# Rows in the order (step, batch) for a fused attention, LSTM and FFN kernel: half of a token chain and seven of eight causal chunks placed inside the recurrence

## Chip, cores and metric

One NeuronCore of a Trainium2 chip runs the whole program. The metric is the device time of one execution in microseconds; the median of three runs of the kernel before is 687.82 us (687.6 to 689.17).

## What is computed

`x` is (4, 256, 128), `cond` (4, 128). Cut to its data flow:

```python
ada = cond @ w_ada + b_ada                       # 6 parts of 128, one set per batch
xm  = expmap0(layer_norm(logmap0(x)) * (1 + sc_msa) + sh_msa)
q, k, v = (to_heads(plin(xm, w, b)) for w, b in ...)     # 16 heads of 8
attn = softmax(logmap0(q) @ logmap0(k).T / sqrt(8))      # no mask: all 256 keys
x1  = mobius_add(x, expmap0(g_msa * logmap0(plin(from_heads(expmap0(attn @ logmap0(v))), w_o, b_o))))
xm  = expmap0(layer_norm(logmap0(x1)) * (1 + sc_mlp) + sh_mlp)
c   = mobius_add(x1, expmap0(g_mlp * logmap0(plin(plin(xm, w_f1, b_f1), w_f2, b_f2))))
x   = x + causal_attention(c)                            # low rank, c @ W_dkv @ W_uk and so on
a_t = x_t @ Wx + b + h @ Wh                              # 256 steps, 4 rows, h from cond, c = 0
c   = sigmoid(f) * c + sigmoid(i) * tanh(g);  h = sigmoid(o) * tanh(c)
out = x + gelu(h @ w1 + b1) @ w2 + b2
```

with `expmap0(v) = tanh(|v|) v / |v|`, `logmap0(x) = arctanh(|x|) x / |x|`, `plin(x, w, b) = expmap0(logmap0(x) @ w + b)`. The chain from the first attention's output to `c` acts on each token by itself. Step t of the recurrence needs `c` for tokens 0 to t of each batch, and nothing later.

## The kernel before

Each engine has one instruction list, written by hand; the lists meet through semaphores. The 1024 tokens lie in 8 tiles of 128 rows, tile 2b+k holding tokens 128k to 128k+127 of batch b.

- **Tables and statistics.** DVE takes the statistics of `x` (L675, L678), scales `ada_b` (L685), copies `cond` out of PSUM (L689). PE makes the six ada parts for each batch, one matmul with `ada_b` and one with `ada_w` into each bank (L1024, L1025), ACT copies them out (L525). Tiles are then turned (L1034) and multiplied by w_q, w_k, w_v (L1043). POOL, at the same time, clears `q_slab` (L450) and builds masks.
- **Head norms** (DVE L806 to L829), a split of q and k into f16 high and low parts (L838, L840), 64 turns (L1051), copies (ACT qS, DVE kS L843). Sixteen DMAs of SP put qS into the zeroed slab `q_slab`, a head's rows in a block of its own, so that all 128 rows can be contracted.
- **Attention 1.** 16 units of (group of four heads, batch): scores (L1066), exp on ACT (L554), values into four 32-column tiles of the array (L1078), turn back (L1089), `o_norm` on DVE.
- **The chain on all 8 tiles**: projection, `join` (L762), `front` (L714), two FFN products (L1137 to L1153), `join` again. Roots are Ln and Exp on ACT (`root`, L490 and L493) with three DVE instructions behind (`rsqrt`, L697 to L699); Ln, Exp and Tanh make ACT load tables (L515, L577).
- **Causal attention.** q, k, v (L1192's inputs; `qz` is filled by 16 more DMAs after POOL has cleared it, L459), then 16 first-half groups of units before the recurrence: scores L1192 and mask L1200, `m_max` L916, exp L611, four 128x128 turns on PE (L1210) and their copy (L923), values L1223, `m_norm`. The second half's units run inside the recurrence, one each 3 steps, through `pe_jobs`, `vec_jobs`, `act_jobs`.
- **Recurrence.** A step: gates on ACT (L642); DVE `pr` (L997), `h_fac` (L999), `gates` (L1001, the new cell); tanh on ACT (L644); DVE `h_off` (L1004), `h_low` (L1006) and `v_tm` (L1008, h for the FFN), then that step's jobs; on PE twelve matmuls (L1358) with `wha`, `whb` on `h_off` and `wha` on `h_low`, then that step's jobs. Each 32 steps the next inputs are made in the four last steps (`inputs_of`, L1242); the FFN pieces (`ffn_up` L1301, `ffn_down` L1316 and L1319, gelu L624) follow from the middle on.

What is queued behind `h_off` on PE, or stands in front of `pr` or `h_off` on DVE, is run first: a job is never overtaken.

Of the kernel before, what the change touches and what calls it, by code (L numbers as in the profile page):

```python
# [28 lines left out]
BF16 = mybir.dt.bfloat16  # L29

B, S, D, H = 4, 256, 128, 16
HD = D // H
FF = 512
P = 128
# [6 lines left out]

# [14 lines left out]
def _beta(a, b):  # L56
# [11 lines left out]
(X_SQ, ARG, IS_SMALL, LN_MINUS, LN_PLUS, N_SQ, ALPHA, V_FACTOR, NORM_SQ, U_NORM,  # L68
 XY, TANH_N, Y_FACTOR, Y_SQ, X_WEIGHT, U_WEIGHT, DENOM, F1_FACTOR, ROOT, NEWTON, GUARDED) = range(21)
SMALL_COLS = 21  # L70
# [8 lines left out]
BIAS_ROWS = BF16_PARTS * 4  # L79


def adaln_attention_lstm_ffn(nc, x, cond, w_q, b_q, w_k, b_k, w_v, b_v, w_o, b_o, w_f1, b_f1, w_f2, b_f2,
                             w_ada, b_ada, W_dq, W_uq, W_dkv, W_uk, W_uv, W_o, Wx, Wh, b_g, w1, b1, w2, b2, out):
    with ExitStack() as ctx:
# [19 lines left out]
        ada_b = sb("ada_b", [1, 6 * D])  # L104
        ada = sb("ada", [P, B, 6, D])
# [5 lines left out]
        bf1_all = sb("bf1_all", [P, FF])  # L111
# [9 lines left out]


# [8 lines left out]
        b2s = sb("b2s", [1, D])  # L131
        x_tb = sb("x_tb", [P, CHUNKS, D])


# [4 lines left out]
        x1_tm = sb("x1_tm", [P, TILES, D])  # L139
        o_tm = sb("o_tm", [P, TILES, D])  # L140
# [3 lines left out]
        qT = sb("qT", [P, TILES, P])  # L144
        kT = sb("kT", [P, TILES, P])
        qz = sb("qz", [P, H, B * S])


        pairs = qz[:].rearrange("p h n -> p (h n)").bitcast(F16)
        kS, qS = (pairs[:, i * NG * B * S:(i + 1) * NG * B * S].rearrange("p (g n) -> p g n", g=NG) for i in range(2))  # L150
        k_pair, q_pair = (pairs[:, i * TILES * H * SLOTS * HD:(i + 1) * TILES * H * SLOTS * HD].rearrange(
            "p (t h s d) -> p (t h) s d", t=TILES, s=SLOTS, d=HD) for i in range(2, 4))

        q_slab = pairs[:, H * B * S:].rearrange("p (h n) -> p h n", h=H)
        vaug = sb("vaug", [P, TILES, H, VP])
        hn = sb("hn", [P, 3, TILES, H])
        p_mla = sb("p_mla", [P, 2, 512])

        p_cond = [a[:].rearrange("p a t h d -> p a (t h d)")[:, i, :] for a in (q_sq, q_tm) for i in range(3)]
        oTs = sb("oTs", [P, 2, S])  # L160
        rd = sb("rd", [P, 2, HALVES, GROUP])
        rdm = sb("rdm", [P, 2, GROUP])
        small = sb("small", [P, SMALL_COLS, TILES])
# [46 lines left out]
        ada_ready = [sem("ada_msa_ready"), sem("ada_rest_ready")]  # L210
# [4 lines left out]
        v_ready = sem("v_ready")  # L215
# [104 lines left out]
        def flat(a):  # L320
            return a.rearrange("p t n -> p (t n)")
# [1074 lines left out]
```

## Time and profile before

| | |
|---|---|
| median of 3 runs | 687.82 us |
| the profiled execution: its span, first to last instruction (no other time is given for it) | 692.0 us |
| span against the median | 4.2 us more |
| start of the first gates, start of the last | 260.6 us, 683.8 us |
| busy PE, DVE, ACT, POOL | 463.2, 407.9, 234.5, 45.7 us |
| mean granted TensorE clock | 0.707 |

The profile's page gives busy shares of the whole span; the views by window, by line and by time give a stage. "idle before, releaser" is how long the engine sat before an instruction, and what it waited for last. An f32 matmul is recorded as two instructions, so "x8" of L1024 is four matmuls. The clock column is the granted share of TensorE's full 2.4 GHz.

### The profile page before, as it was taken

Reading aid. Unit: us, or ns where it says so; the run is one execution under the profiler, and the core shown is the slowest. Engines: PE = TensorE matmul, PEld = TensorE weight load, DVE = VectorE, ACT = ScalarE, POOL = GpSimd, SP = SyncE. Lnnn points to the kernel's source line nnn. Section 1 sums busy time; section 2 is a strip of 40 time slices with the busy share of each in tenths; the row PEclk is TensorE's granted clock in tenths of the full one; section 3 lists DMA queues with packets and bytes.
Section 4 is the critical chain, followed back from the end, with each engine's and each line's share of the span. In section 5 each row is a group of like instructions: output and inputs, shape, how many; then the busy total and the mean of one; then the engine's idle time right before and its main releaser. Section 6 shows DMA issues by size and latency. Waiting matters only on the chain.

```text
span 692.0 us, 13536 instructions
## 1 busy us (share of the span) xinstructions
PE 463.2 (67%) x5003; PEld 318.3 (46%) x5003; DVE 407.9 (59%) x2108; ACT 234.5 (34%) x818; POOL 45.7 (7%) x41
## 2 busy tenths in 40 slices
PE   0593799104839979888899889737367367367346
PEld 0231433102616756665566567536256246256334
DVE  6458533896674865767766775654444544544443
ACT  0023787232333523333433432223222232222222
POOL 9500002530000000000000000000000000000000
PEclk9997799655959985999985995555555555555555
DMA  7100200000002000000000000000000000000000
GB/s 188 45 0 0 61 2 2 0 0 0 1 0 32 1 1 2 1 3 1 2 1 3 1 2 1 2 1 1 5 6 2 5 6 1 5 5 3 5 1 5
DMA packets 9312, 7.00 MB, mean 10 GB/s; under 512 B 1845, under 2 KB 8093, under 8 KB 9246
## 3 DMA queue, kind: packets, MB, share of 16 engines
q1 hardware_dynamic: 8206, 5.60, 3.5%
q8 instruction: 40, 0.66, 0.4%
q10 hardware_dynamic: 1040, 0.52, 0.3%
q14 instruction: 26, 0.21, 0.1%
HBM read 4.02 MB, written 0.52 MB: 7 GB/s over the span
## 4 chain that ended last, share of the span: by engine, by line
PE 44%; DVE 36%; ACT 14%; issue 5%; DMA 1%; DVEq 0%
PE bank L1358 13%; ACT h_fac L644 6%; DVE h_off L1004 5%; PE bank L1192 5%; DVE pr L997 4%; ACT gates L642 4%; DVE gates L1001 4%; PE bank L1223 3%; PE bank L1078 3%; PE bank L1210 3%; DVE h_fac L999 2%; PE bank L1066 2%; DVE mx L916 2%; DVE q_sq L923 2%; DVE ada_b L685 2%
## 5 line engine op out<-in xcount | busy, mean ns | idle before, releaser
L1358 PE MATMUL bank<-h_off,wha 128*128 128x4 f16 x1020 | 68.3, 171 | 121.9 <-DVE h_off L1004 118.5
L1358 PEld LDWEIGHTS bank<-h_off,wha 128*128 128x128 f16 x1020 | 50.5, 106 | 166.4 <-DVE h_off L1004 160.7
L642 ACT ACTIVATE gates<-bank 128x16 f32<-128x16 f32 x256 | 46.9, 183 | 192.2 <-PE bank L1358 191.1
L997 DVE SCALAR_TENSOR_TENSOR pr<-gates 128x8 f32<-128x8 f32 x256 | 42.1, 164 | 106.3 <-ACT gates L642 106.3
L644 ACT ACTIVATE h_fac<-gates 128x4 f32<-128x4 f32 x256 | 53.1, 207 | 110.0 <-DVE gates L1001 110.0
L1004 DVE TENSOR_TENSOR h_off<-h_fac 128x4 f16<-128x4 f32 x256 | 43.3, 169 | 70.0 <-ACT h_fac L644 70.0
L1192 PE MATMUL bank<-kT,qz 128*128 128x128 f32 (+1 forms) x256 | 71.4, 394 | 0.0
L1358 PE MATMUL bank<-h_low,wha 128*128 128x4 f16 x1020 | 63.8, 167 | 0.0
L1358 PE MATMUL bank<-h_off,whb 128*128 128x4 f16 x1020 | 62.5, 166 | 0.0
L1006 DVE TENSOR_TENSOR_SCAN h_low<-h_fac,h_off 128x12 f16<-128x12 f32 x256 | 46.7, 183 | 8.7
L611 ACT ACTIVATE p_mla<-bank,mx 128x128 f32<-128x128 f32 (+1 forms) x128 | 44.4, 414 | 18.1 <-DVE mx L916 18.1
L1223 PE MATMUL bank<-q_sq,vaug 128*32 128x128 f32 x384 | 46.2, 312 | 1.9 <-DVE oTs L929 1.9
L1358 PEld LDWEIGHTS bank<-h_off,whb 128*128 128x128 f16 x1020 | 46.1, 101 | 0.0
L1358 PEld LDWEIGHTS bank<-h_low,wha 128*128 128x128 f16 x1020 | 45.8, 103 | 0.0
L1192 PEld LDWEIGHTS bank<-kT,qz 128*128 128x128 f32 x256 | 38.8, 209 | 7.1 <-issue 7.0
L1210 PE MATMUL bank<-ident,p_mla 128*128 128x128 f32 x192 | 41.3, 315 | 0.9 <-ACT p_mla L611 0.9
L999 DVE TENSOR_SCALAR h_fac<-gates 128x4 f32<-128x4 f32 x256 | 41.3, 161 | 0.0
L1001 DVE SCALAR_TENSOR_TENSOR gates<-pr 128x4 f32<-128x4 f32 x256 | 41.3, 161 | 0.0
L1008 DVE TENSOR_TENSOR v_tm<-h_fac 128x4 f32<-128x4 f32 x256 | 37.1, 145 | 0.0
L923 DVE COPY q_sq<-bank 128x512 f32<-128x512 f32 x48 | 32.9, 686 | 5.2 <-PE bank L1210 5.2
L916 DVE TENSOR_REDUCE mx<-bank 128x2 f32<-128x512 f32 (+1 forms) x48 | 32.9, 686 | 4.8 <-PE bank L1200 4.6
L1210 PEld LDWEIGHTS bank<-ident,p_mla 128*128 128x128 f32 x192 | 24.1, 157 | 9.4 <-issue 5.5
(224 smaller groups left out, 737.9 us busy)
## 6 DMA issues: line engine op xcount, KB each, us to landing
qz<-qz SPq DMA_DIRECT2D x16, 64.0 KB, 2.0
x_tm<-in_x ACTq DMA_DIRECT2D x1, 512.0 KB, 5.0
wf<-in_L_cond_w_f SPq DMA_DIRECT2D x2, 256.0 KB, 5.7
x_tb<-in_x SPq DMA_DIRECT2D x4, 128.0 KB, 2.7
qz<-qT SPq DMA_DIRECT2D x16, 32.0 KB
out_y<-tb SPq DMA_DIRECT2D x7, 64.0 KB, 1.9
ada_w<-in_L_cond_w_ada SPq DMA_DIRECT2D x1, 384.0 KB
bf_all<-in_L_cond_b_f SPq DMA_DIRECT2D x1, 256.0 KB, 5.8
```

The costliest lines, as they stand in the source:

```text
L642: nc.scalar.activation(gates[:, k, 0:GW], src, ACT.Tanh, scale=1.0 / A_SCALE).then_inc(gates_act, 1)
L644: nc.scalar.activation(h_fac[:, k, :, 1], gates[:, 1 - k, 4 * B:5 * B], ACT.Tanh, scale=0.5).then_inc(th_act, 1)
L916: V.tensor_reduce(mx[:, m % 2, 0:512 // n], bank[:, m % 2, :].rearrange("p (j n) -> p j n", n=n), AX.X, ALU.max, negate=True).then_inc(mx_ ...
L923: V.tensor_copy(pt_mla[:, m % 2, :], bank[:, 2 + m % 2, :]).then_inc(mt_ready, 1)
L997: V.scalar_tensor_tensor(pr[:, k, :], gates[:, k, B:3 * B], 1.0, gates[:, k, 3 * B:5 * B], ALU.add, ALU.mult).then_inc(p_ready, 1)
L999: V.tensor_scalar(h_fac[:, k, :, 2], gates[:, k, 0:B], 1.0, 0.5 * H_SCALE, ALU.add, ALU.mult)
L1001: V.scalar_tensor_tensor(gates[:, 1 - k, 4 * B:5 * B], pr[:, k, B:2 * B], 0.5, pr[:, k, 0:B], ALU.mult, ALU.add).then_inc(c_new, 1)
L1004: V.tensor_tensor(h_off[:, k, :, 2], h_fac[:, k, :, 2], h_fac[:, k, :, 1], ALU.mult).then_inc(h_ready, 1)
L1192: T.matmul(bank[:, m % 2, j * n:(j + 1) * n], qz[:, h, b * S + half * P:b * S + half * P + P], kT_flat[:, b * S:b * S + n], start=(j == 0) ...
L1210: ins = T.transpose(bank[:, 2 + m % 2, i * P:(i + 1) * P], p_mla[:, m % 2, i * P:(i + 1) * P], ident[:])
L1223: ins = T.matmul(bank[VP * j:VP * j + VP, 4, 0:P], vaug[:, HALVES * b + kc, h, :], pt_mla[:, m % 2, i * P:(i + 1) * P], start=(kc == 0), s ...
L1358: ins = T.matmul(acc[:, g * B:(g + 1) * B], w[:, g, :], h, start=False, stop=True, skip_group_check=True)
```

## The change

The chain on half k (tokens 128k and on) becomes a generator `side(k)` per engine. `side(0)` runs among the second 16 units of attention 1 and after them; `side(1)` is carried as far as tables of step numbers say (`VEC_AT`, `ACT_AT`, `PE_AT`, `Pace`), most of it inside steps 0 to about 70. Its tiles are 32 steps by 4 batches (`x_tb` order), so a tile is one chunk of causal attention (`attend(c, i)`); chunk 0 comes ahead of the recurrence, chunks 1 to 7 inside.

```diff
+CHUNK_FROM = {1: 0, 2: 20, 3: 40, 4: 64, 5: 88, 6: 112, 7: 136}
+VEC_AT = dict(second=0, joined=0, log1=12, log2=15, moved=25, v_ready=36, squared0=38, squared1=40, squared2=42, squared3=45,
+              f1_factor=49, fed=53, third=60, fourth=65)
+PE_AT = dict(projected=30, v_turned=33, up0=34, up1=37, up2=39, up3=43, normed=45)
...
-            for k, (a, z) in enumerate(ADA_PARTS):
...
-                    T.matmul(y, ones[:], ada_b[:, a:z], start=True, stop=False)
-                    ins = T.matmul(y, condR[:, bb], ada_w[:, a:z], start=False, stop=True)
+            for bb in range(B):
+                ins = T.matmul(bank[:, 1 + bb // 2, bb % 2 * 2 * D:(bb % 2 + 1) * 2 * D], condR[:, bb], ada_w[:, 0:2 * D], start=True, stop=True)
...
+            T.matmul(bank[:, 3, :], condS[:].rearrange("p t b -> p (t b)"), ada_w[:, 2 * D:6 * D], start=True, stop=True).then_inc(ada_mm, 1)
```

(`ada_b` is now spread over 128 rows by a DMA of ACT's queue and added on DVE as the tables are copied out.) POOL no longer clears `q_slab` and `qz`, and SP's 32 DMAs into them are gone; folding of the second attention's weights, the turns of `x_tb` and the product with `Wx` move ahead of attention 1.

```diff
 # attention 1, scores and values
-                    ins = T.matmul(bank[:, 2 * (w % 2) + kc, :], kS[:, g, ...],
-                                   q_slab[:, h:h + 2, bb * S:(bb + 1) * S], start=True, stop=True)
+                        ins = T.matmul(bank[:, 2 * (w % 2) + j % 2, i * P:(i + 1) * P], kS[rows, g, ...],
+                                       qS[rows, g, bb * S + k * P:bb * S + (k + 1) * P], start=True, stop=True,
+                                       tile_position=(SLOTS * HD * j, 0), skip_group_check=True)
 # a root: was Ln and Exp on ACT and three DVE instructions
+                    on(V.tensor_scalar(at(y).bitcast(I32), at(a).bitcast(I32), -0.5, ROOT_BITS, ALU.mult, ALU.add))
+                    on(V.tensor_tensor(at(T1), at(a), at(y), ALU.mult))
+                    on(V.scalar_tensor_tensor(at(T1), at(T1), -ROOT_K, at(y), ALU.mult, ALU.mult))
+                    on(V.scalar_tensor_tensor(at(T2), at(T1), ROOT_C, at(y), ALU.add, ALU.mult))
+                    on(V.tensor_tensor(at(T1), at(a), at(T2), ALU.mult))
+                    on(V.scalar_tensor_tensor(at(T1), at(T1), -1.0 / ROOT_S ** 2, at(T2), ALU.mult, ALU.mult))
+                    on(V.scalar_tensor_tensor(at(Y), at(T1), 10.0 / 3.0, at(T1), ALU.add, ALU.mult))
+                    on(V.scalar_tensor_tensor(at(y), at(Y), 5.0, at(T2), ALU.add, ALU.mult))
 # causal attention: turns of p
-                    ins = T.transpose(bank[:, 2 + m % 2, i * P:(i + 1) * P], p_mla[:, m % 2, i * P:(i + 1) * P], ident[:])
+                V.transpose(pt_mla[:, m % 2, n * part:n * (part + 1)], p_mla[:, m % 2, n * part:n * (part + 1)]).then_inc(mt_ready, 1)
 # the recurrence on DVE
                 V.scalar_tensor_tensor(gates[:, 1 - k, 4 * B:5 * B], ...).then_inc(c_new, 1)
+                rest.go(t, 1)
                 vec.wait_ge(th_act, t + 1)
                 V.tensor_tensor(h_off[:, k, :, 2], h_fac[:, k, :, 2], h_fac[:, k, :, 1], ALU.mult).then_inc(h_ready, 1)
...
-                for job in vec_jobs(t):
-                    job()
+                for c, i in attending(t):
+                    attend(c, i)
+                    jobs += 1
+                rest.go(t, 3 if jobs == 0 else 2)
```

A log is now bits, a fit and two Exp steps, so ACT needs no Ln. The diff of PE's causal scores: one matmul of 32(c+1) columns for four heads (32 rows of the array) and a 32-column mask matmul; its values: 36-column matmuls on a block-diagonal V (`vbd`), four batches in four 32-column tiles. The twelve matmuls and six DVE instructions of a step are the same (now L1622 and L1291 to L1302; gates L760, tanh L762). `hist` is what `v_tm` was.

Where instructions move, on PE in attention 1. Before, scores and values alternate by batch (`qz` is the storage that the slab and kS share, `vaug` V, `q_sq` and `q_tm` exponentials):

```order
L1066 MATMUL bank<-qz 128x512 x2
L1078 MATMUL bank<-q_sq,vaug 32x256 x4
L1066 MATMUL bank<-qz 128x512 x2
L1078 MATMUL bank<-q_sq,vaug 32x256 x2
L1078 MATMUL bank<-q_tm,vaug 32x256 x2
```

and now, in the second 16 units, with half 0's turns and projection (L1422, L1427, L1434) between:

```order
L1398 MATMUL bank<-q_tm,vaug 32x128 x8
L1427 MATMUL bank<-ident,o_tm 128x128 x4
L1380 MATMUL bank<-qS,kS 128x128 x8
L1398 MATMUL bank<-q_tm,vaug 32x128 x8
L1434 MATMUL bank<-wo_c,vT 128x128 x4
L1380 MATMUL bank<-qS,kS 128x128 x8
```

One score product of 512 columns on the full array has become four of 128 columns on a quarter of its rows.

PE in the recurrence, steps 34 to 37. Before, a step that turns and takes values (L1210, L1223), then scores:

```order
L1358 MATMUL bank<-h_low,wha 128x4 x4
L1210 MATMUL bank<-ident,p_mla 128x128 x3
L1223 MATMUL bank<-q_sq,vaug 32x128 x3
L1358 MATMUL bank<-h_off,wha 128x4 x4
L1358 MATMUL bank<-h_off,whb 128x4 x4
L1358 MATMUL bank<-h_low,wha 128x4 x4
L1223 MATMUL bank<-q_sq,vaug 32x128
L1192 MATMUL bank<-kT,qz 128x256
L1197 MATMUL bank<-mask,identb 128x128
```

and now (L1446 is the first FFN product of half 1, L1496 a chunk's values):

```order
L1622 MATMUL bank<-h_low,wha 128x4 x4
L1478 MATMUL bank<-kT,qz 128x96
L1480 MATMUL bank<-mask,sel 128x32
L1478 MATMUL bank<-kT,qz 128x96
L1480 MATMUL bank<-mask,sel 128x32
L1622 MATMUL bank<-h_off,wha 128x4 x4
L1622 MATMUL bank<-h_off,whb 128x4 x4
L1622 MATMUL bank<-h_low,wha 128x4 x4
L1496 MATMUL bank<-vbd,pt_mla 32x36 x12
L1446 MATMUL bank<-vT,wf 128x512
L1622 MATMUL bank<-h_off,wha 128x4 x4
```

The step's own matmuls keep their order; what stands behind `h_low` is other work.

DVE in a step, before with a causal unit's two jobs, and now with a chunk's and the chain's (L1109 the chain, L1247 a turn of p):

```order
L1001 SCALAR_TENSOR_TENSOR gates<-pr 128x4
L1004 TENSOR_TENSOR h_off<-h_fac 128x4
L1006 SCALAR_TENSOR_TENSOR h_low<-h_fac,h_off 128x12
L1008 TENSOR_TENSOR v_tm<-h_fac 128x4
L923 COPY q_sq<-bank 128x512
```

```order
L1294 SCALAR_TENSOR_TENSOR gates<-pr 128x4
L1109 SCALAR_TENSOR_TENSOR sm<-sm 128x4
L1298 TENSOR_TENSOR h_off<-h_fac 128x4
L1300 SCALAR_TENSOR_TENSOR h_low<-h_fac,h_off 128x12
L1302 TENSOR_TENSOR hist<-h_fac 128x4
L1247 STREAM_TRANSPOSE pt_mla<-p_mla 128x128
L1109 SCALAR_TENSOR_TENSOR sm<-sm 128x4 x2
```

A chain instruction now stands between the new cell and `h_off`, where there was none.

## Rows read from the trace of the kernel before

**Rows 1.** Busy time in stretches: span; engines; granted clock; DMA share, GB/s.
```profile
0.00:53.70 53.70, 28.98 (x47) 11.02 (x48) 30.14 (x71) 8.21 (x19) 26.22 (x33) 1.00 0.30 75
53.70:79.40 25.70, 10.28 (x76) 7.73 (x74) 21.53 (x35) 13.04 (x18) 0.00 (x0) 0.67 0.05 12
79.40:121.20 41.80, 40.29 (x358) 13.22 (x356) 13.46 (x50) 33.10 (x33) 3.82 (x1) 1.00 0.08 19
121.20:205.40 84.20, 28.46 (x155) 20.14 (x155) 66.37 (x204) 26.39 (x66) 15.67 (x8) 0.65 0.00 0
...
260.60:683.80 423.20, 300.33 (x3936) 225.53 (x3937) 241.44 (x1651) 131.44 (x608) 0.00 (x0) 0.63 0.01 3
683.80:692.00 8.20, 4.91 (x20) 3.27 (x20) 1.27 (x8) 1.20 (x6) 0.00 (x0) 0.50 0.04 10
```
**Rows 2.** The same, two stretches of the recurrence.
```profile
280.00:340.00 60.00, 52.17 (x691) 35.99 (x690) 43.89 (x267) 23.39 (x100) 0.00 (x0) 1.00 0.01 2
...
415.00:450.00 35.00, 31.29 (x323) 21.09 (x321) 20.81 (x129) 10.11 (x45) 0.00 (x0) 0.50 0.01 1
```
**Rows 3.** Timeline, one step without jobs: start, duration (us), engine, idle before, releaser.
```profile
500.89 0.19 PEld L1358 LDWEIGHTS bank<-h_off,wha 128*128 128x128 f16 x4 [1.20 <-DVE h_off L1004]
...
501.41 0.18 ACT L642 ACTIVATE gates<-bank 128x16 f32<-128x16 f32 x1 [0.78 <-PE bank L1358]
501.63 0.17 DVE L997 SCALAR_TENSOR_TENSOR pr<-gates 128x8 f32<-128x8 f32 x1 [0.51 <-ACT gates L642]
...
502.26 0.17 DVE L1004 TENSOR_TENSOR h_off<-h_fac 128x4 f16<-128x4 f32 x1 [0.27 <-ACT h_fac L644]
```
**Rows 4.** Timeline, a step whose PE jobs are long.
```profile
441.53 1.06 PE L1223 MATMUL bank<-q_sq,vaug 128*32 128x128 f32 x6
...
442.52 0.18 PEld L1358 LDWEIGHTS bank<-h_off,wha 128*128 128x128 f16 x4 [0.38 <-issue]
...
443.04 0.18 ACT L642 ACTIVATE gates<-bank 128x16 f32<-128x16 f32 x1 [1.33 <-PE bank L1358]
```
**Rows 5.** Timeline of DVE, the start.
```profile
5.72 1.64 DVE L675 BATCH_NORM_STATS2 st<-x_tm 128x6 f32<-128x128 f32 x8 [5.72 <-DMA x_tm<-in_x]
```
**Rows 6.** Groups of instructions by line and form, 0 to 53.7 us.
```profile
L450 POOL MEMSET qz<- 128x1024 f16 x16 | 14.4, 947 | 0.0
L685 DVE TENSOR_SCALAR ada_b<-ada_b 1x128 f32<-1x128 f32 x1 | 13.7, 13666 | 0.0
```
**Rows 7.** Timeline of PE, the ada tables.
```profile
24.36 1.22 PE L1024 MATMUL bank<-ada_b,ones 1*128 1x256 f32 x2 [18.09 <-DVE condR L689]
...
33.56 2.07 PE L1024 MATMUL bank<-ada_b,ones 1*128 1x512 f32 x2
```
**Rows 8.** Timeline, attention 1.
```profile
90.51 0.11 PEld L1066 LDWEIGHTS bank<-qz 128*128 128x128 f16 x2 [0.41 <-issue]
...
91.05 0.64 PE L1078 MATMUL bank<-q_sq,vaug 128*32 128x256 f32 x8
...
92.52 1.02 ACT L554 ACTIVATE q_tm<-bank 128x1024 f32<-128x1024 f32 x1 [0.34 <-PE bank L1066]
```
**Rows 9.** Timeline of DVE, the chain's first join.
```profile
125.91 5.25 DVE L764 TENSOR_SCALAR small<-small 128x8 f32<-128x8 f32 x1
131.74 0.17 DVE L697 TENSOR_TENSOR small<-small 128x8 f32<-128x8 f32 x1 [0.58 <-ACT small L493]
131.94 0.17 DVE L698 SCALAR_TENSOR_TENSOR small<-small 128x8 f32<-128x8 f32 x1
...
132.55 2.19 DVE L768 SCALAR_TENSOR_TENSOR ta<-ta,small,ada 128x128 f32<-128x128 f32 x8
```
**Rows 10.** Groups by line and form, 262 to 450 us.
```profile
L916 DVE TENSOR_REDUCE mx<-bank 128x2 f32<-128x512 f32 x32 | 21.9, 683 | 0.0
...
L929 DVE COPY oTs<-bank 128x128 f32<-128x128 f32 x15 | 4.2, 283 | 0.0
```
**Rows 11.** Timeline, the first step's matmuls, with the unsplit f32 `wh`.
```profile
258.84 1.71 PE L1358 MATMUL bank<-h,wh 128*128 128x4 f32 x8
```

More of the change, by code:

```diff
@@ new lines, in _ @@
+            exps(0, PER_HALF)
+            exps(16, 18)
+            first, second = side(0), side(1)
+            until(first, "turned")
+            exps(18, 19)
+            until(first, "first")
+            exps(19, 20)
+            until(first, "second")
+            o_copy(0)
+            exps(20, 22)
+            until(first, "bent")
+            exps(22, 24)
+            o_copy(1)
+            exps(24, 27)
+            until(first, "log1")
+            exps(27, 28)
+            until(first, "log2")
@@ L574, in _ @@
+            for i in range(chunk_span(0)):
+                attend(0, i)
+                if i == 8:
+                    until(second, "second")
             act.wait_ge(w_ready, 6)
@@ L802, in _ @@
+            for k in range(2):
+                vec.wait_ge(sq_out, 1 + k)
+                go(V.tensor_reduce(half(col(V_FACTOR), k), half(tb, k), AX.X, ALU.add))
+            done()
+            step(V.tensor_scalar(col(GUARDED), col(V_FACTOR), TINY, None, ALU.max), roots_in)
+            rsqrt(col(GUARDED), col(V_FACTOR), col(NEWTON))
+            step(V.tensor_scalar(col(V_FACTOR), col(V_FACTOR), CLIP, 1.0, ALU.mult, ALU.min))
             vec.wait_ge(ld_qkv, 96)
@@ new lines, in _ @@
+            until(first, "v_ready")
+            for f in range(FC):
+                until(first, f"squared{f}")
+                if f == 1:
+                    until(second, "normed0")
+            until(second, "normed1")
+            until(first, "f1_factor")
+            until(first, "fed")
+            until(second, "normed3")
+            until(first, "fourth")
+            until(second, "added")
+            until(first, "end")
+            go(V.memset(h_fac[:], 0.0))
+            go(V.memset(h_off[:], 0.0))
@@ L962, in _ @@
+            for i in range(chunk_span(0)):
+                attend(0, i)
+            until(second, "second")
             step(V.memset(gates[:], 0.0), c_new)
@@ L1263, in _ @@
-            pe.wait_ge(mv_ready, 1)
+            pe.wait_ge(kT_ready, NG)
+            pe.wait_ge(qT_ready, NG)
+            pe.wait_ge(vaug_ready, 1)
+            first, second = side(0), side(1)
+            scores(0)
+            scores(1)
+            for g in range(NG):
+                units(PER_GROUP * g, PER_GROUP * g + 2)
+                if g:
+                    until(first, f"turn{g - 1}")
+                units(PER_GROUP * g + 2, PER_GROUP * (g + 1))
+            until(first, f"turn{NG - 1}")
```

1578 lines of the change are left out of this document (907 added, 671 removed).

## Prediction

> **What bounds the kernel now.** I read the stretches first, then the timeline of one step, then groups and timelines of the earlier stages. The stretches [rows 1] split the span of 692.0 us in two: 260.6 us before the first gates, and 423.2 us for 255 intervals of the recurrence, with a tail of 8.2 us. Outside attention 1 no engine fills the first part: DVE is the busiest, with 66.4 of the 84.2 us of the token chain, where small instructions follow each other; PE has 28.5 there. That work can only be shortened or put where an engine idles. The reader is to see in a step without jobs [rows 3] where it idles: the gates repeat after 1.60 us whatever the clock, because each engine waits for the next; PE stood idle for 1.20 us (1.27 from its last h matmul to the next `h_off` by my reading of start times), ACT .78, DVE .51 ahead of `pr` and .27 ahead of `h_off`. Over 255 intervals PE alone has some 320 us of room. An interval is prolonged only by what exceeds such a gap: the job of 1.06 us in [rows 4], begun late, holds the h matmuls ([0.38 <-issue]) and the next gates come 1.33 us after the last ACT work in place of .78. All intervals together exceed 255 x 1.594 = 406.5 us by 16.7, all of it in stretches at clock .50: in one at 1.00, with PE busy for 52.2 of 60 us, none did [rows 2]. So the sum is: time to the first gates, plus 406.5, plus overruns, plus tail.
>
> **The tables (a gain of 28).** Now PE's first table product waits until 24.4 [rows 7] for DVE's scaling of `ada_b`, which took 13.7 us beside POOL's 16 memsets of 14.4 us [rows 6]; these are removed. In the new order the statistics and copies end at about 10.1 (x lands at 5.7 and its statistics take 1.64 [rows 5]; then .64 for their sums, three copies and small work). Then four products of 256 columns at 1.15 (eight of them from 24.36 to 33.56) and one of 512 at 2.0 [rows 7], where sixteen took 25.1, give 16.7; sums with the bias, normalisation and turns 9 us. QKV starts at 25.7 for 53.7: -28.
>
> **Up to attention 1 (+1.5).** The 25.7 us of this stretch [rows 1] keep their DVE work; ten weight turns and products go into PE's idle 15 us. Their ACT and DVE copies, and 2.7 us of statistics of `x_tb`, stand ahead of the last k copies. Start of the scores: 53.3.
>
> **Attention 1, first half and its output (31).** Each half has 16 exps of 1.02 us [rows 8], so ACT needs 16.4. PE's values of a (group, batch) cost .55 twice for four column tiles at a time (91.05 to the next score product, less its gap). Now eight matmuls of 128 columns alternate between two of the tiles, which I take as two at a time: .85; scores on 32 rows .21 to .43. With the gaps of both changes 1.3 us per unit, 21; fill 4; the last turns, norm, turn and projection 6. The chain's input stands at 84.2. A score product contracted 128 rows before, three quarters of them zeros of the slab; now 32.
>
> A rule speaks against this part. The row shows PE idle for .41 us at issue where 32-column values give way to scores [rows 8], and the same .38 in the recurrence [rows 4]; both are in my 1.3. The Trainium skill ("TensorEngine Tiling (Array Packing)", section Key Properties) says that a change of tiling mode, not of tile, drains TensorE. By that rule each tiled job in the recurrence pays a change too: the overruns counted below at half clock are 65 us with .25 us for each such step, and 57 without, so the sum would be 6 us lower if the rule did not hold here. This case's rows agree in that the gap stands at the change, but cannot tell it from a weight load's wait.
>
> **The chain for four tiles (75).** Small chained instructions repeat each .20 us, 128x8 or less alike [rows 9]; per-tile ones cost 2.19 / 8 = .275. The collision with POOL's memset of `qz` (5.25 us for an instruction of .17) goes. A root was two ACT instructions with two crossings (.58 of the second is seen in [rows 9]) and three on DVE, some 1.3 us, and is now eight on DVE: 1.6. The removed table loads I cost at nothing, as ACT waits there. Join: 33 small, 16 per-tile, one reduction and squares with crossings: 13.5. Front: 48 small, 8 per-tile, 8 of statistics and two Exp crossings: 12.5. Clip and scaling 4.4. FFN: two products of four tiles, at 2.19 per tile and a factor: 15.4; the second half's `o_norm` lies between. Join again 13.7. Ends at 143.7; the second half's first part, 12 small and 8 per-tile, which is not overlapped, 5.1: 148.8.
>
> **Chunk 0 (9) and entry (4).** Four units, each a round of scores, maximum, exp, turns and values of some 2.2 us when nothing else runs, behind one tile's turn and projections: reductions of up to .68 [rows 10], turns of p on DVE. No row before has such a turn; between .28 (copy of 128x128) and .68 (128x512) [rows 10], I take .28, the same shape. Then norm, turn, inputs 1.8, and `wh` 1.71 [rows 11]. First gates: 162 for 260.6, 99 earlier; 157 at full clock.
>
> **The recurrence.** 406.5 stays. I added, per step of the new lists, PE's jobs against 1.27, DVE's behind `hist` against .51, its one instruction ahead of `h_off` (.20 to .22) against .27, ACT's against .80. Prices: a 512-column f32 product 1.7 to 2.0 at half clock (by [rows 7], whose pace is that of the long jobs at .50) and half of that at full; 128 columns f32 .35 ([rows 4], three in 1.06) to .43; small DVE work .20. Overruns: 65 us at half clock, of which 31 by t = 63 (there each of 4 up products of 1.7 and 16 + 16 narrow f32 ones meets chunk 1's and 2's scores), 16 in t 64 to 159 and 18 behind; 32 at full clock, mostly DVE's. In it .25 in each step with tiled matmuls stands for the gap at issue, below the .38 seen; without it the half-clock count is 57. The clock was .50 in most of the recurrence before [rows 1], mean .63, though at 1.00 in the loaded stretch. By that mean three quarters of steps go at half clock: 56. But jobs that come late in one step leave the next with more room, which a sum by step does not see: before, such a sum would have given more than the 16.7 found. I take 48. Tail: the last piece is unchanged, 8.2.
>
> **Sum.** 162 + 406.5 + 48 + 8.2 = 624.7 us of span. The profiled execution before has 692.0 against a median of 687.8, so I take off 4.2: **620.5 us**, 67 less.
>
> **Rivals.**
> (a) *The clock stays up in the loaded stretches.* For it: [rows 2] 1.00 for 60 us with causal work. Against: the new steps carry less PE work each. Then entry at 157 and overruns near 32: 157 + 406.5 + 32 + 8.2 - 4.2 = 600.
> (b) *Half clock throughout, nothing absorbed.* All of 65: 637.5. If also the value tiles of attention 1 run one after another, 1.70 for .85 over 16 units, 13 more: 651. For it: PE is idler than before; against: the 16.7 of before.
> (c) *Slower.* The chain's instruction between the new cell and `h_off`, and the waits at the head of chunk jobs, stand in the path of each step: DVE's list cannot pass them. If such an instruction waits for PE or ACT work that is itself queued behind the h matmuls, each affected interval grows by up to an engine round, .8 us. To bring back 67 us on top of the 48, a mean of .26 us over all 255 intervals is needed, or .8 us in 84 of them. Against: chunks are active in most steps, but their waits are two or more steps after the producer, and the DVE gap holds .20 in .27. Then 620.5 + 67 + 1 = 689.
> (d) *The recurrence absorbs it, the front does not:* stream turns of .68, tiny tiled matmuls at issue cost, chunk 0 and the log's crossings at twice my price: +15: 636.
> (e) *The chain of half 1 is not hidden, only moved.* Alone it takes 75 us as half 0's; if none fits the gaps, its 31 us of overruns before t = 64 become 75: 664. Against: .20 in .27 and three times .20 against .51 leave only .1 over per step.
>
> **How the numbers follow.** My case .44, (a) .2, (b) .15, (d) .14, (e) .02, (c) .05, of which .01 ends within the noise. A measurement here tells about 0.3%, 2 us. The range that leaves 2 in 10 out: down to 597 (case (a) with its entry costs a little lower), up to 648, between the two ends of (b). Faster .95, same .01, slower .04, as every case but (c) is over 30 us to that side.
>
> **What would show it.** First gates near 162; QKV from 25.7; no POOL memset beside DVE's first instructions; an attention unit of 1.3 us; gates 1.60 apart in steps without jobs; overruns in t 33 to 50 and at steps with 4c score columns, released by PE at clock .50. I am wrong if first gates lie 10 us off, if intervals without PE overrun still exceed 1.65 (then DVE's inserted instruction is in the path), or if the stretch of t 75 to 250 adds more than 35 us.

## The result and the profile after

The changed kernel takes **647.08 us** (median of 4, 645.41 to 648.18) where the kernel before took 688.50 in the same comparison; ratio .9382, interval .9356 to .9409. That is 41 us less; 67 were forecast (620.5 us), and the value lies 1 us inside the range's upper end. On three later chips the kernel before took 676 to 682 us in 7 of 25 executions and 687 to 695 us in the others, so the four here are of its longer kind, and against the shorter ones the changed kernel gains 32 us (645.7 for 677.9 on one chip, ratio .9519, interval .9478 to .9561), less than half of the 67 forecast.

The page, and below it the stretches of the profile after (span, PE, PEld, DVE, ACT, POOL busy, clock), which answer to [rows 1]:

```profile
span 644.5 us, 16323 instructions
...
PE 489.7 (76%) x6317; PEld 383.3 (59%) x6317; DVE 385.3 (60%) x2265; ACT 239.7 (37%) x928; POOL 20.5 (3%) x31
...
PEclk9567996886555555565555555555565555556555
```

```profile
0.00:26.30 26.30, 6.67 (x19) 4.46 (x20) 22.60 (x74) 4.24 (x11) 13.28 (x25) 0.82 0.58 158
26.30:54.00 27.70, 15.55 (x62) 9.71 (x63) 25.05 (x43) 16.84 (x31) 6.09 (x5) 0.62 0.00 1
...
85.00:130.00 45.00, 32.59 (x394) 22.89 (x392) 25.49 (x131) 21.61 (x49) 0.00 (x0) 0.77 0.01 1
130.00:177.80 47.80, 35.02 (x248) 29.79 (x242) 28.36 (x126) 16.69 (x73) 1.15 (x1) 0.67 0.00 1
177.80:636.30 458.50, 367.77 (x5138) 292.31 (x5138) 273.78 (x1860) 159.25 (x742) 0.00 (x0) 0.51 0.01 3
636.30:644.50 8.20, 4.85 (x20) 3.21 (x19) 1.07 (x7) 1.15 (x6) 0.00 (x0) 0.50 0.01 2
```

The last three numbers of a stretch are clock, DMA share and GB/s. An interval is the time from one step's gates to the next step's, and its overrun is what it has above the 1.594 us of a step without jobs. The first gates come at 177.8 us, not 260.6: 82.8 us earlier, of 99 forecast. The recurrence takes 458.5 us for 423.2, so 35.3 us are given back: its overruns are 52.0 us for 16.7. The tail is the same 8.2. So the change took about 83 us out of the front and paid back 35 inside, which is the shape that was forecast. The mean clock of the recurrence is .51, where it was .63.

Where the 52.0 us stand can be read from the start times of each step. Some 35 us lie between `h_off` and PE's first h matmul, where PE is still at a job. Some 11 us lie ahead of `pr`, where DVE is still at its own jobs, and 2.7 us ahead of `h_off`, behind the chain's inserted instruction.

Two long intervals show how the work is paid for. First PE, at step 43, with half 1's norm products of one column:

```profile
257.63 0.25 PE L1622 MATMUL bank<-h_low,wha 128*128 128x4 f16 x4
257.80 0.59 PE L1496 MATMUL bank<-vbd,pt_mla 128*32 128x36 f32 x24
259.23 0.27 PE L1622 MATMUL bank<-h_off,wha 128*128 128x4 f16 x4 [0.84 <-DVE h_off L1298]
259.36 0.25 PE L1622 MATMUL bank<-h_off,whb 128*128 128x4 f16 x4
259.47 0.25 PE L1622 MATMUL bank<-h_low,wha 128*128 128x4 f16 x4
259.56 3.49 PEld L1452 LDWEIGHTS bank<-ones,q_pair 128*128 128x128 f32 x16
259.58 3.55 PE L1452 MATMUL bank<-ones,q_pair 128*128 128x1 f32 x16
262.99 0.25 PE L1622 MATMUL bank<-h_off,wha 128*128 128x4 f16 x4
```

Twelve value matmuls of 36 columns (257.80) leave PE idle for .84 us before the next step. Eight products of one column (259.58, two records each) take 3.55 us, .43 each, and the weight queue is busy for 3.49 us of that, so one column costs what 128 do in the prediction (.35 to .43), and the rows point to the loading of the 128x128 weights. The next h matmuls wait for them and the interval is 3.73 us. Then step 34, where causal scores and a first FFN product (L1446) meet:

```profile
240.19 2.08 PE L1446 MATMUL bank<-vT,wf 128*128 128x512 f32 x2
242.05 0.29 PE L1622 MATMUL bank<-h_off,wha 128*128 128x4 f16 x4
...
242.60 0.18 ACT L760 ACTIVATE gates<-bank 128x16 f32<-128x16 f32 x1 [1.94 <-PE bank L1622]
242.81 0.17 DVE L1291 SCALAR_TENSOR_TENSOR pr<-gates 128x8 f32<-128x8 f32 x1 [2.50 <-ACT gates L760]
```

ACT and DVE both wait behind PE, DVE 2.50 us for .51 in [rows 3]. The interval is 3.59 us.

The overruns of the kernels are compared in the table at the end of the experiments.

### The profile page after: what moved, and what is told of

Read it like the earlier page. It is cut to its first block, busy times and chain, and to the rows that moved or that the text cites. A ratio compares the mean times of both kernels' runs of the same rounds, so it can differ in the third digit from the quotient of the medians.

```text
span 644.5 us, 16323 instructions
## 1 busy us (share of the span) xinstructions
PE 489.7 (76%) x6317; PEld 383.3 (59%) x6317; DVE 385.3 (60%) x2265; ACT 239.7 (37%) x928; POOL 20.5 (3%) x31
## 4 chain that ended last, share of the span: by engine, by line
PE 44%; DVE 33%; ACT 16%; issue 5%; DMA 1%; PEldq 0%; ACTq 0%; DVEq 0%
PE bank L1622 14%; PE bank L1478 6%; ACT h_fac L762 6%; DVE h_off L1298 5%; ACT gates L760 5%; DVE pr L1291 4%; PE bank L1398 4%; DVE gates L1294 4%; DVE h_fac L1292 2%; DVE mx L1237 2%; PE bank L1518 2%; DVE pt_mla L1247 2%; PE bank L1446 2%; PE bank L1380 2%; PE bank L1460 2%
## 5 line engine op out<-in xcount | busy, mean ns | idle before, releaser
L1622 PEld LDWEIGHTS bank<-h_off,wha 128*128 128x128 f16 x1020 | 52.0, 109 | 145.2 <-DVE h_off L1298 135.8
L1622 PE MATMUL bank<-h_off,wha 128*128 128x4 f16 x1020 | 68.9, 172 | 84.0 <-DVE h_off L1298 80.0
L760 ACT ACTIVATE gates<-bank 128x16 f32<-128x16 f32 x256 | 47.2, 185 | 181.2 <-PE bank L1622 181.0
L1291 DVE SCALAR_TENSOR_TENSOR pr<-gates 128x8 f32<-128x8 f32 x256 | 41.5, 162 | 112.4 <-ACT gates L760 111.6
L1478 PE MATMUL bank<-kT,qz 32*128 32x32 f32 (+7 forms) x256 | 105.8, 534 | 0.0
L762 ACT ACTIVATE h_fac<-gates 128x4 f32<-128x4 f32 x256 | 53.1, 207 | 120.2 <-DVE gates L1294 120.2
L1478 PEld LDWEIGHTS bank<-kT,qz 32*128 32x128 f32 x256 | 63.6, 311 | 3.1 <-issue 1.1
L1622 PE MATMUL bank<-h_low,wha 128*128 128x4 f16 x1020 | 63.4, 167 | 0.0
L1622 PE MATMUL bank<-h_off,whb 128*128 128x4 f16 x1020 | 62.7, 166 | 0.0
L1622 PEld LDWEIGHTS bank<-h_low,wha 128*128 128x128 f16 x1020 | 46.8, 104 | 0.0
L1622 PEld LDWEIGHTS bank<-h_off,whb 128*128 128x128 f16 x1020 | 46.7, 103 | 0.0
L706 ACT ACTIVATE p_mla<-bank,mx 128x32 f32<-128x32 f32 (+7 forms) x128 | 43.3, 368 | 6.0 <-DVE mx L1237 6.0
L1496 PE MATMUL bank<-vbd,pt_mla 128*32 128x36 f32 x1152 | 40.0, 254 | 4.7 <-ACT qS L731 3.8
L1302 DVE TENSOR_TENSOR hist<-h_fac 128x4 f32<-128x4 f32 x256 | 37.1, 145 | 0.0
L1247 DVE STREAM_TRANSPOSE pt_mla<-p_mla 128x192 f32<-128x192 f32 (+5 forms) x96 | 35.5, 369 | 2.0 <-ACT p_mla L706 1.7
L1496 PEld LDWEIGHTS bank<-vbd,pt_mla 128*32 128x32 f32 x1152 | 33.0, 157 | 6.0 <-issue 4.0
L1237 DVE TENSOR_REDUCE mx<-bank 128x2 f32<-128x320 f32 (+7 forms) x48 | 26.3, 549 | 3.9 <-PE bank L1480 3.7
L1480 PE MATMUL bank<-mask,sel 32*128 32x32 bf16 x128 | 28.6, 225 | 0.0
```

The costliest lines, as they stand in the source:

```text
L706: ins = nc.scalar.activation(p_mla[:, m % 2, i * n:(i + 1) * n], bank[:, 3 + m % 2, i * n:(i + 1) * n], ACT.Exp, bias=mx[:, m % 2, i:i + 1])
L760: nc.scalar.activation(gates[:, k, 0:GW], src, ACT.Tanh, scale=1.0 / A_SCALE).then_inc(gates_act, 1)
L762: nc.scalar.activation(h_fac[:, k, :, 1], gates[:, 1 - k, 4 * B:5 * B], ACT.Tanh, scale=0.5).then_inc(th_act, 1)
L1247: V.transpose(pt_mla[:, m % 2, n * part:n * (part + 1)], p_mla[:, m % 2, n * part:n * (part + 1)]).then_inc(mt_ready, 1)
L1291: V.scalar_tensor_tensor(pr[:, k, :], gates[:, k, B:3 * B], 1.0, gates[:, k, 3 * B:5 * B], ALU.add, ALU.mult).then_inc(p_ready, 1)
L1478: T.matmul(bank[:, 3 + m % 2, i * n:(i + 1) * n], qz[rows, c % 2, bs[i]].rearrange("p j t -> p (j t)"), kT[rows, bs[i], 0:n], start=(i == ...
```

## Experiments

Twelve runs on three chips; those of one group share a chip: e1 to e4, e5 to e8, e9 to e12. The program's time is its span plus 1.8 us, in all executions but two of e7 (2.3 and 3.2). Executions of one changed kernel lay 1 to 12 us apart. So the kernels are compared by their own intervals, and by medians against the changed kernel's 645.7 (e9) to 647.1. The changed kernel was run beside e10 to e12 alone: for e1 to e8 a difference of 1 to 3 us between medians is not told apart from one between chips, and the overruns decide.

**e1, the instruction ahead of `h_off` taken away.**

```diff
-                rest.go(t, 1)
-
                 vec.wait_ge(th_act, t + 1)
...
-                rest.go(t, 3 if jobs == 0 else 2)
+                rest.go(t, 4 if jobs == 0 else 3)
```

> The chain's one DVE instruction between the new cell and h_off is taken away; all of the chain's DVE work stands behind hist (up to 4 instructions a step). Overrun theory (PE jobs at half clock): the gap ahead of h_off holds .20 in .27, so nothing is won there, and four chained instructions of .20 exceed the .51 behind hist by .3 in some 35 steps: 5 to 12 us slower than the changed kernel (652 to 659 us). Rival (the inserted instruction stands in the path): steps 0 to 70 get shorter, 5 us or more faster (below 642 us).

Measured 648.11 us (645.39 to 651.63), overruns 55.7 for 52.0, and all the increase is in t below 96. On the whole the instruction is cheaper where it stood, and nothing like the loss of rival (c) is there. DVE of the changed kernel, a step with it:

```profile
196.05 0.16 DVE L1294 SCALAR_TENSOR_TENSOR gates<-pr 128x4 f32<-128x4 f32 x1
196.13 0.15 DVE L1102 SCALAR_TENSOR_TENSOR sm<-sm 128x4 f32<-128x4 f32 x1
196.49 0.17 DVE L1298 TENSOR_TENSOR h_off<-h_fac 128x4 f16<-128x4 f32 x1 [0.20 <-ACT h_fac L762]
```

DVE still waits .20 for tanh behind it (.27 without), so a small instruction is free there. A large one is not. In step 36 a product of 128x512 stands in that place:

```profile
244.71 0.16 DVE L1294 SCALAR_TENSOR_TENSOR gates<-pr 128x4 f32<-128x4 f32 x1
244.79 0.68 DVE L1180 TENSOR_TENSOR q_pair<-k_pair 128x512 f32<-128x512 f32 x1
245.39 0.16 DVE L1298 TENSOR_TENSOR h_off<-h_fac 128x4 f16<-128x4 f32 x1
```

Tanh starts at 244.91, so `h_off` follows it by .48 us for the usual .24. In e1 steps 36, 38, 40 and 42 fall from 1.84 to between 1.60 and 1.69, and step 49 from 2.25 to 1.59. Rival (c)'s mechanism is real in nine steps of the changed kernel, and costs 2.7 us there. In e1 these 2.7 are gone, but the waits ahead of `pr` grow by some 7 us. The loss was forecast too high, 5 to 12 us for 3.7 by the overruns.

**e2, values over two steps.**

```diff
+                    if c and (kb <= c // 2) != (half == 0):
+                        continue
...
-                    m_values(c, u)
+                    m_values(c, u, 0)
+                if c and w == 1 and 0 <= u < unit_count(c):
+                    m_values(c, u, 1)
```

> A causal unit's value matmuls of chunks 1 to 7 are spread over two steps, half of the key blocks in each. Overrun theory: the 10 longest steps behind t = 64 (2.3 to 3.15 us, some 11 us over) are value jobs that meet another job; halved, 6 to 10 us less than the changed kernel (637 to 641 us). Rival (waits between engines, not PE's load, make these steps long): within 2 us of 647.

647.73 us (646.96 to 650.17), overruns 56.1. The longest steps fell (134: 2.99 to 2.63 us, 162: 3.11 to 2.75), but steps that had been at 1.6 now took 1.9 to 2.2, for the second half lands where the next unit's scores are. The expectation was wrong: I had looked at peaks. A cycle of three steps has 3.8 us of room, and PE is recorded busy for 45.5 of the 50 us from 450 to 500 us, which holds the first of these steps.

**e3, POOL's bias work after k's turns.**

```diff
+            pool.wait_ge(k_turned, NG)
             pool.wait_ge(w_ready, 4)
```

> POOL's six bias conversions wait until k is turned, and so no longer run beside DVE's q, k and v products (1.39 us for .56, 3.61 for 2.36, 1.62 for 1.22). Theory that POOL slows DVE there: 2.5 us less, 644.5 us, first gates 2.5 us earlier. Rival (the long durations are the instructions' own): no change, and DVE's rows as before.

644.27 us (640.03 to 646.63), first gates at 174.2. DVE and POOL, in the changed kernel and then in e3:

```profile
42.08 1.17 POOL L517 TENSOR_TENSOR bg<-bg,p_mla 1x512 f32<-1x512 f32 x1
42.28 1.39 DVE L901 SCALAR_TENSOR_TENSOR hn<-hn,nq 128x384 f32<-128x384 f32 x1
43.70 3.61 DVE L904 SCALAR_TENSOR_TENSOR q_tm<-q_tm,hn 128x1024 f32<-128x1024 f32 x2
47.23 1.62 DVE L907 TENSOR_TENSOR vaug<-q_tm,hn 128x1024 f32<-128x1024 f32 x1
```

```profile
41.99 0.56 DVE L902 SCALAR_TENSOR_TENSOR hn<-hn,nq 128x384 f32<-128x384 f32 x1
42.59 2.36 DVE L905 SCALAR_TENSOR_TENSOR q_tm<-q_tm,hn 128x1024 f32<-128x1024 f32 x2
44.87 1.22 DVE L908 TENSOR_TENSOR vaug<-q_tm,hn 128x1024 f32<-128x1024 f32 x1
55.58 0.60 POOL L515 CAST p_mla<-bg 1x512 bf16<-1x512 f32 x1 [40.07 <-PE bank L1369]
```

The same three instructions take 4.1 us for 6.6, and the split of k into high and low parts starts at 48.20 for 50.98. The change removed POOL's long memsets from DVE's side and put small POOL work beside these three products. The DVE rows show 2.5 to 2.8 us; the rest of the earlier gates is within what one profile differs from another (175 to 180 us over the other kernels), and the median alone, on another chip, would not show it.

**e4 and e5, the clock.** Filler matmuls on PE in steps 60 to 189, into a bank that nothing reads there (e4: 128 columns each; e5: 512 columns, with `wha` in place of the second `identh`, the sum of jobs and filler higher).

```diff
+                for _ in range(FILL[t]):
+                    T.matmul(bank[:, 0, 0:P], identh[:], identh[:], start=True, stop=True, skip_group_check=True)
```

> In steps 60 to 189 PE's idle time behind the jobs is filled with matmuls of 128 columns f16 on the identity into an unused bank (up to 10 of .107 us, so that jobs and filler come to some 1.15 us at half clock). Nothing of the result changes. Theory that idleness keeps the clock at .50: it rises to 1.00 in a part of that stretch, and its overruns (some 20 us at half clock) fall to some 10: 637 us. Rival (the clock does not follow such work): clock .50 as before, and no change or up to 5 us slower from filler that begins late.

> As the last filler, but with matmuls of 512 columns on the full array, so that jobs and filler of a step in 60 to 189 come to 1.75 us at half clock, above the 1.27 of room. Theory that the clock follows the columns that PE moves: it rises to 1.00 as it did in 280 to 340 us of the kernel before; then filler and jobs fit the room, that stretch's overruns fall from 21 to some 10 us, and the sum is near 637. Rival (the clock stays at .50 in this stretch whatever PE does): each of 130 intervals grows by up to .5 us, 690 us or more.

e4: 648.13 us, e5: 669.2 us (664.71 to 676.77). Stretches of the changed kernel, e4 and e5:

```profile
320.00:360.00 40.00, 29.88 (x432) 23.49 (x432) 22.97 (x161) 13.29 (x63) 0.00 (x0) 0.50 0.01 1
450.00:500.00 50.00, 45.51 (x668) 34.43 (x666) 31.21 (x191) 17.63 (x77) 0.00 (x0) 0.53 0.01 2
```

```profile
320.00:360.00 40.00, 38.84 (x528) 32.59 (x525) 22.40 (x157) 12.76 (x61) 0.00 (x0) 0.50 0.01 2
450.00:500.00 50.00, 47.86 (x681) 36.58 (x681) 30.38 (x188) 17.91 (x78) 0.00 (x0) 0.50 0.01 2
```

```profile
320.00:360.00 40.00, 37.96 (x523) 22.71 (x521) 23.81 (x166) 13.68 (x65) 0.00 (x0) 0.98 0.01 2
450.00:500.00 50.00, 49.54 (x635) 32.78 (x632) 28.04 (x175) 15.94 (x70) 0.00 (x0) 0.64 0.01 2
```

With the wide filler the clock did go up, to .98 in 320 to 360 us, and there the steps between 74 and 101 were all within 1.7 us though they carry more work (in the changed kernel step 78 takes 2.28 and step 92 takes 1.99). With the narrow one, for which PE is recorded just as busy, it stayed at .50, and e4's rival held. But with the wide filler the clock was down to .78 in 360 to 400 us, then .64 and .50, and then the filler itself overran: t 128 to 191 went from 13.1 us to 29.4. So the clock of this recurrence can be raised for a while, but not kept up, and not at this price. Both theories of e5 were too simple: it was neither 637 nor over 690.

**e6, chain first in ACT's and PE's lists ahead of the recurrence.**

```diff
-            exps(24, 27)
-            until(first, "log1")
-            exps(27, 28)
-            until(first, "log2")
+            exps(24, 25)
+            until(first, "log1")
+            exps(25, 26)
+            until(first, "log2")
+            exps(26, 28)
...
-            units(18, 31)
+            units(18, 29)
             until(first, "v_turned")
             until(first, "up1")
-            units(31, 32)
+            units(29, 32)
```

> ACT's exps of the second half of attention 1 stand behind the chain's two log exps where they stood ahead of them, and PE turns half 0's chain and makes its first FFN products ahead of the last three units, not behind all but one. Theory that chain and attention hold each other up in the two lists (DVE waits of 2.64 and .78 us for ACT, 7.6 us ahead of the squares): first gates 3 to 5 us earlier than 177.8, 642 to 644 us. Rival (PE's and ACT's sums bound this stretch, whatever the order): within 1 us.

644.49 us (643.33 to 646.73) but first gates at 178.4, not earlier: the rival held, as far as one profile can tell. It is the profile of the longest of e6's four executions, and the others were 1.3 to 3.4 us shorter, so a small gain is not excluded. Waits moved from the log to the FFN: DVE's wait of 2.64 us is gone, and the one of 7.59 ahead of the squares is 9.72.

**e7, half 1's FFN spread over more steps** (each first product in two of 256 columns, four norm matmuls a step, two second products a step, later tables, `CHUNK_FROM` 70, 94, 118, 142, `FFN_EVERY` 7).

```diff
-CHUNK_FROM = {1: 0, 2: 20, 3: 40, 4: 64, 5: 88, 6: 112, 7: 136}
+CHUNK_FROM = {1: 0, 2: 20, 3: 40, 4: 70, 5: 94, 6: 118, 7: 142}
...
+                            if k and f == 1:
+                                yield
```

> Half 1's FFN products in steps 33 to 54: each first product in two of 256 columns in two steps, four norm matmuls a step for eight, two second products a step for four; what follows of the chain and chunks 4 to 7 come 6 steps later. The matmul work is the same. Overrun theory: the six steps of 2.8 to 3.84 us (34, 37, 39, 43, 44, 46; 10.7 us over) fall to about 2.2 each, others rise by .3: 4 to 7 us less, overruns of t 32 to 63 near 12 for 17.4; 641 to 643 us. Rival (PE's sum over these 20 steps is full, as the split of the values showed behind t = 64): no gain, 645 to 649.

650.04 us (649.38 to 653.14), overruns 57.0, t 32 to 63 21.1 for 17.4. Steps 43 and 44 did fall to 2.03 and 2.13, and 50 and 55 rose to 4.07 and 3.81, where parts meet chunk 2's and 3's. The rival held, and there was a loss beside.

**e8, masks behind pairs of scores.**

```diff
                              start=(i == 0), stop=True, skip_group_check=True, tile_position=(32 * g, 0))
+                for i in range(len(bs) // 2 * part, len(bs) // 2 * (part + 1)):
                     ins = T.matmul(...sel32[rows, :], mask32[rows, :], ...)
```

> Two causal score matmuls, then their two masks, where score and mask alternate; same work. In chunk 0 a pair of 32 columns repeats each .48 us though its columns are few. Theory that the change between f32 scores and bf16 masks costs (a drain at each): chunk 0 shorter by up to 2 us and two changes fewer in each score step of the recurrence, 3 to 6 us less in all. Rival (the pair is bound by its three weight loads, .18 to .33 each): no change within 1 us.

643.05 us (642.55 to 644.35), overruns 51.0. PE in chunk 0 of the changed kernel, then of e8:

```profile
163.31 0.61 PE L1478 MATMUL bank<-kT,qz 32*128 32x32 f32 x2
163.73 0.21 PE L1480 MATMUL bank<-mask,sel 32*128 32x32 bf16 x1
163.79 0.61 PE L1478 MATMUL bank<-kT,qz 32*128 32x32 f32 x2
```

```profile
161.71 0.44 PE L1519 MATMUL bank<-w_mla,coT 128*32 128x128 f32 x4
162.08 1.06 PE L1478 MATMUL bank<-kT,qz 32*128 32x32 f32 x4
...
163.03 1.06 PE L1478 MATMUL bank<-kT,qz 32*128 32x32 f32 x6
```

A pair takes .48 us alternating and .95 us for two in e8: the same. Changing between f32 and bf16 costs nothing in chunk 0. That the price is the three weight loads of a pair is the rival's reading, and no run tests it. In the recurrence the order matters a little: steps 34 and 37 fell by .14 each and steps 51, 52, 55, 64 and 65 by .2, step 47 rose by .5, and all overruns fell by 1.0. What the median shows beyond that is not explained by a row.

**e9 to e12.** e9 is the changed kernel itself. In e10 DVE adds the four squared blocks, and 4 norm products replace 16; the tables move them to step 45:

```diff
+                        ins = V.tensor_tensor(f1q[:, 0], f1q[:, 0], f1q[:, f], ALU.add)
...
-                for f in range(FC):
-                    pe.wait_ge(f1_sq, FC * k + f + 1)
-                    for c in range(SIDE):
+                pe.wait_ge(f1_sq, k + 1)
+                for c in range(SIDE):
```

e11 is e10 with e3's and e8's edits. In e12 PE makes only a stub of half 1's FFN inside the recurrence, and leaves the rest of it out:

```diff
+                    n = 16 if k else 4 * P
...
-                    for c in range(SIDE):
+                    for c in range(1 if k else SIDE):
...
-                    for f in range(FC):
+                    for f in range(1 if k else FC):
```

> The changed kernel as it is, beside the three below on one chip. By every theory as before: 645 to 648 us, overruns of the 255 intervals 52 us.

> The squares of the FFN's four blocks are added on DVE (three adds of .69 us for each half), so that PE makes 4 norm products with one column in place of 16, .43 us each at half clock. Same result up to rounding. Overrun theory: steps 43 and 44 (3.73 and 3.84 us) fall to one of some 2.3, 3 to 4 us less in t 32 to 63, of which DVE's adds give back about .5; before the recurrence 16 products of .23 us become 4, up to 2 us more less DVE's three adds (2.1 us, if they are in the path). Sum: 2 to 5 us less than the changed kernel beside it. Rival (the room is used up everywhere, what leaves one step comes back in the next, as with the two splits): within 1 us.

> Norms summed, the pairs of masks behind the pairs of scores, and POOL's bias work after k is turned, together. If the three add up: 6 to 9 us less than the changed kernel beside it, near 639 us.

> Half 1's FFN is left out on PE but for a stub in the recurrence (first products of 16 columns for 512, 4 norm matmuls for 16, 4 second products for 16); its result is wrong. Overrun theory: t 32 to 63 fall from 17.4 us over to about 5, the rest unchanged: 12 us less than the changed kernel. Rival (the chain's DVE and ACT work or waits on it are what prolongs these steps): 3 us less at most.

| | median us (range) | first gates | overruns, us | of which t 32 to 63 |
|---|---|---|---|---|
| before | 677.89 (677.47 to 680.75) in three, 690.45 (687.80 to 690.82) in eight | 260.6 | 16.7 | 1.0 |
| changed, first time | 647.08 (645.41 to 648.18) | 177.8 | 52.0 | 17.4 |
| e9 changed | 645.69 (643.78 to 648.26) | 176.8 | 52.0 | 17.4 |
| e10 norms summed | 642.47 (640.49 to 644.04) | 175.5 | 48.5 | 13.8 |
| e11 all three | 635.90 (631.65 to 641.12) | 176.9 | 47.1 | 13.3 |
| e12 stub | 635.86 (633.73 to 637.81) | 179.3 | 42.0 | 7.7 |

(First gates and overruns are from one profile each; those of before from the first one.) e9 repeats the overruns to a tenth. e12 shows that half 1's FFN on PE is 9.7 of the 17.4 us of steps 32 to 63 (forecast: about 12), and its median is 9.8 us below e9's. e10 turns two steps of 3.73 and 3.84 into 2.32 and 2.63 and is 3.2 us faster by medians, within the 2 to 5 forecast; its step 45, with four norm products behind a unit's values:

```profile
261.16 0.25 PE L1626 MATMUL bank<-h_low,wha 128*128 128x4 f16 x4
261.34 0.58 PE L1500 MATMUL bank<-vbd,pt_mla 128*32 128x36 f32 x24
261.86 1.87 PE L1458 MATMUL bank<-ones,q_pair 128*128 128x1 f32 x8
263.58 0.25 PE L1626 MATMUL bank<-h_off,wha 128*128 128x4 f16 x4
```

**e11 beats both kernels**: 635.9 us, 9.8 less than the changed one beside it (6 to 9 forecast) and 42 to 55 less than the kernel before. Each of its six executions is shorter than each of the changed kernel's six. Its overruns give 4.9 of the 9.8 and POOL's place some 2.7, if it is worth there what it was in e3; the last two are not shown by a row, and its profiled execution (638.8 us of span) was one of its longer ones.

## Why the prediction was right, and by how much it was off

**The mechanism holds, the number only just.** The front is shorter, the recurrence is prolonged mostly by PE jobs at clock .50, and the base step and the tail are untouched. But the time is 27 us above the forecast, and it is inside the range by 1 us only because the range reached up to the middle of rival (b), whose serial value tiles did not come. That is luck. Two of the prediction's own signs of being wrong came true: the first gates lie 15.8 us off, where 10 were allowed, and 37 intervals exceed 1.65 us though PE was not late (11.9 us of overrun, nearly all behind DVE's work). The 27 us fall on three terms.

**The front, 15.8 us too small.** *Tables*: QKV at 26.3 for a forecast of 25.7. *Up to attention 1*: scores at 58.5 for 53.3; I costed DVE's products at their old durations and did not see POOL's bias work move beside them, which e3 measures at 2.5 to 2.8 us. The other 2 us of this stretch are not accounted for. *Attention 1*: 33.0 us for 30.9; a unit is 1.33 us at full clock, as taken, and the value matmuls do overlap (1.07 us for eight, between the .85 taken and the 1.70 of rival (b)), but one unit, at half clock, took 2.4 us, and each fourth is followed by turns. *The chain*: its heading says 75 us, and rival (e) uses that number, but its parts and the sum (84.2 to 148.8) come to 64.6. It took 71.4, from 91.5 to 162.9. Both joins and the second half's part were right within .2 us. The front took 15.7 us for 12.5 and the FFN 19.6 for 15.4. I had summed DVE's instructions and PE's products as if alone, while the second half of attention 1 stands between them in the same lists:

```profile
109.60 0.94 DVE L1109 SCALAR_TENSOR_TENSOR sm<-sm 128x4 f32<-128x4 f32 x5
113.18 0.16 DVE L1114 TENSOR_TENSOR sm<-sm 128x4 f32<-128x4 f32 x1 [2.64 <-ACT sm L637]
...
114.79 0.16 DVE L1127 TENSOR_TENSOR sm<-sm 128x4 f32<-128x4 f32 x1 [0.78 <-ACT sm L637]
...
132.20 1.42 DVE L1180 TENSOR_TENSOR q_pair<-k_pair 128x512 f32<-128x512 f32 x2 [7.59 <-ACT k_pair L651]
```

DVE waits 2.64 us for an Exp of .22 that stands behind three attention exps, 2.88 us together, in ACT's list. That e6 moves these waits and its first gates come no earlier suggests that the two streams together bound this stretch. Chunk 0 and the entry took 14.8 us for 13.2. Rival (d) had 15 us more for the front, which is the size that came, but for other reasons: the turns of p took .24 in chunk 0, not .68, and of its reasons only the log's crossings are in these rows.

**The recurrence, 4 us.** 52.0 against 48. The count by steps was 65 us at half clock with an allowance for a change of tiling, and 57 without. Two choices failed in opposite ways. The clock was not high for a quarter of the steps but for almost none (.51), so it is case (b) in the clock. And the allowance of .25 us for a change of mode was not there. I had read [.41 <-issue] and [.38 <-issue] in [rows 4, 8] as PE's idle time; it stands in the row of the weight queue. PE itself went on: in the trace before, the score product that begins at 90.51 is recorded for .61 us, and the values of [rows 8] start at 91.05, while it is still at work. In the changed kernel values on 32 columns follow `h_low` by .17 us (257.63 to 257.80), where a product on the full array follows it by .11 (259.47 to 259.58), and scores on 32 rows start while the last projection on 32-column tiles is recorded (161.71 + .44, and 162.08, in e8). The rule of the Trainium skill ("TensorEngine Tiling (Array Packing)", Key Properties) that a change of tiling mode drains TensorE may hold, but by these rows the change to tiles costs some .06 us, not .25; no row separates the change back.

The count with the allowance had 31 us by t = 63, 16 in t 64 to 159 and 18 behind; the trace has 23.7, 14.7 and 13.6. Without the allowance 5 us remain between 57 and 52. That late jobs find room in the next step is my reading of them; no run shows it. One cost was taken as nothing and was not: the inserted instruction was counted at .20 to .22 against a gap of .27, but four of them are products of .68 us, and 2.7 us come of such ones (e1).

**The reference to the median, 6.8 us.** I took 4.2 us off the span, because the profiled execution before had 692.0 against a median of 687.8. But an execution's time is its span plus 1.8: that profile was of an execution 6 us above the median. The changed kernel has no execution that far from its median, so the correction had the wrong sign: 1.8 should have been added, not 4.2 taken off, and the changed kernel's median lies .8 above its profiled execution.

**Rivals.** (a) failed, though e5 shows the clock at .98 when PE is given more. (b) came in the clock, but not with its 65 us nor with its serial value tiles. (c) failed in size: its mechanism is there in nine steps, for 2.7 us (e1). (e) failed: with the causal work of the same steps it costs 24 us of overruns up to t = 63, not 75. Of 255 intervals 161 round to 1.6, where 207 did before. The stretch behind t = 75 added some 26 us, under the 35 named.

**Open:** why one execution's first gates come 2 us before another's, why executions of the kernel before lie 12 us and more apart, and what takes the clock down from 360 us on in e5. No run takes the front apart further than e3 and e6 do: how much of the 83 us each removed piece is worth is read from timelines.

## What to carry to other kernels

Work moved into the idle gaps of a recurrence is free only up to the gap of each engine in each step, and a count by steps against these gaps, made from the instruction lists, gave the loss (57 us by the count at half clock, 52 measured); when cycles are full, splitting peaks made it worse (e2, e7) and removing work helped (e10). Look at the size of each instruction that is put ahead of the critical one, not at the usual size. Where two streams share in-order lists ahead of the recurrence, add a term for their waits on each other: sums for each alone were some 7 us short. And look at what POOL does beside DVE's largest instructions after a move.

## What the runs showed of the hardware that was not expected

- An f32 matmul of one column with 128x128 weights took .43 us at clock .50 (3.55 for eight), with the weight queue busy for 3.49 of these 3.55 us.
- DVE's 128x384 product took 1.39 us with a POOL subtraction and a cast of one row beside it, .56 without (e3).
- Filler of 512 columns raised the granted clock from .50 to .98 over 40 us, filler of 128 columns left it at .50, with PE recorded busy for 38.0 and 38.8 of the 40 us (e5, e4).
- A 32-row score of 32 columns with its mask takes .48 us in either order (e8).
- Values on 32-column tiles followed full-array matmuls by .17 us, a full-array product by .11: the change to tiles cost some .06 us.
